# A transformer layer with attention and routed experts on one core: a new order of transfers at the start, and gates stored in pieces of four bytes

## The chip, the cores and the metric

One core of a Trainium2 chip runs the whole kernel. The metric is the device time of one execution in microseconds. A core has TensorE (PE, matrix products into eight PSUM banks), VectorE (DVE), ScalarE (ACT), GpSimd (POOL) and SyncE (SP), each with an instruction list of its own, and 16 DMA engines between DRAM and SBUF. The lists run beside each other and meet at semaphores.

## The reference, cut to what matters

```
x: (8, 512, 128);  xn = layernorm(x)
attention over 16 heads of 8, keys and queries turned by an angle that depends on the batch index:
    scores = q k^T / sqrt(8);  weights = softmax(scores);  att = weights v
router on xn: s = sigmoid(xn gate_w^T); group scores of 8 groups of 4 (sum of the best two of s + e_bias);
    the best 4 groups; in them the best 6 experts of s + e_bias;
    combine = 2.5 * s / sum of the chosen s (zero for the other experts)       (tokens x 32 experts)
moe = sum over e of ((relu(xn up_e^T))^2 * combine_e) down_e^T                 (32 experts, inner 64)
shared = (relu(xn shared_up^T))^2 shared_down^T                                (inner 256)
out = x + att + moe + shared
```

All arithmetic is in fp32.

## The kernel before

**Units and steps.** Each of the 8 batches of 512 tokens is cut into 16 units, so there are 128 units; a unit `u` treats two experts (128 inner columns) of batch `u // 16` and, for attention, four heads and one block of 128 keys (`kt = u % 4`). Four units with the same four heads are a step; there are 32 steps, and a step has 16 score tiles for the row maxima, which run ahead of use by up to 12 tiles (`SC_AT`). In a unit TensorE's list is: the first couple of heads (`couple(u, 0)`: `weights_max` adds the negated maxima as a product of `ones` with `m_rows`, `weights_product` the scores), some score tiles for later maxima, `pv` of the unit before, then at most a few extra products for coming batches (at the unit numbers in the constants `X_UNIT`, `Q_UNIT`, `GATE_UNIT` and so on), the second couple, the down products (`expert_down`, up to two a unit by `DOWN_AT`, from unit 6 on), and the up product (`expert_up`), into the bank `up_b`, which the extra products share.

**The gates.** VectorE computes the router in ten pieces (`route`, at the units in `ROUTE_MID` and `ROUTE_END`; `ROUTE1_*` for batch 1). Its last piece writes `gates`, 128 tokens by 4 tiles by 32 experts. TensorE turns it with four transposes (`gate_transpose`) in unit 12, ScalarE copies the result to `gT` (`gate_out`), SyncE stores it to DRAM as `gate_rows` (experts by tokens, `store_gates`), and after that has landed, loads rows of it, each spread over 64 partitions, into `gate_at` (`load_gates`, one group of four units at a time, two buffers). POOL multiplies: `gated = gate_at * relu`, `g = gated * relu`. ScalarE makes `relu` from `up_b`, and the exponentials `probs` from the banks `st0` and `st1`.

**The stacks.** Queries and keys are split by POOL into a high and a low part (`split`), stored to DRAM (`store_rows`, four transfers of 256 KB each for q and k) and loaded in a stacked form (`load_stack`) as four rows groups per head. A row maximum is cut into three bf16 parts by POOL (`cut_max`), turned by TensorE, copied by ScalarE to `m_parts` and loaded by SyncE as `m_rows` (`load_max`, three small transfers).

**SyncE's order.** All transfers are issued by SyncE in one list, in order, waits included. In step `s` it sends `load_max(s + 1)`, `load_gates(s + 1)`, and, depending on the step, outputs, x and stores for the batch after the next, then `load_stack` for the next batch. `load_stack(1, ...)` waits until all eight stores of batch 1 have landed. For batch 0 the first two steps' stacks are made without DRAM; those of steps 2 and 3 go through it.

**The start.** Before unit 0 TensorE computes 16 score tiles for step 0; after the pair `i` of them it does one other product if `BESIDE` names it, and then six tiles of step 1 with the products in `BEHIND`. ScalarE evacuates in the same order. The exponential's table is loaded by a small `Exp` on `blank` after all of them.

**The end.** After unit 127 come the last down products, the last `pv`, the copy of its result, its turning, the last down product, and on VectorE `att_out`, then `last_sum`: x + att, then the accumulated bank on top.

## Time and profile before

| what | us |
|---|---|
| median of two runs | 665.76 (665.56 to 665.96) |
| the profiled execution | 666.02 |
| its span, from first to last instruction | 664.2 |

Mean granted TensorE clock over the span: 0.981 of full speed. Times in the rows count from the start of the span. In a timeline a row stands for one instruction or for neighbours of the same kind, with their count behind an x; the number in brackets is how long the engine stood idle before it, and what ended that.

### The profile page before, as it was taken

The page shows a single profiled execution, that of the slowest core. Times are in us where ns is not written, and L with a number is a line of the kernel's source. Part 1 is how long each engine was busy: PE and PEld are TensorE (multiplying, and loading weights), DVE is VectorE, ACT ScalarE, POOL GpSimd, SP SyncE. Part 2 cuts the span into 40 slices and gives each one's busy share as a digit, 9 for nine tenths or more (in the row PEclk, how much of TensorE's full clock was granted, in tenths as well). Part 3 has the DMA queues.
Part 4 walks back from the last instruction along what each step waited for, and adds up shares of the span by engine and source line. Part 5 has one row for each costly group of instructions (what it writes and reads, how often), then busy time and mean ns, then how long its engine had stood idle before and what let it go on. Part 6 is the DMA issues. An engine that isn't in the chain of part 4 may idle for free.

```text
span 664.2 us, 12408 instructions
## 1 busy us (share of the span) xinstructions
PE 643.2 (97%) x4320; PEld 297.6 (45%) x4320; DVE 421.3 (63%) x1056; ACT 410.5 (62%) x785; POOL 446.3 (67%) x528
## 2 busy tenths in 40 slices
PE   8897799999999999999999999999999999999996
PEld 5432444454444444444444444444444444444443
DVE  7785677485756767575765757575765867565402
ACT  3564365576666666676667666665676667666653
POOL 6730568876788677876688667875766667566653
PEclk9977799899999999999999999999999999999999
DMA  4444634532546443263545524273544524232420
GB/s 137 136 124 126 137 96 100 163 106 55 142 100 215 106 114 96 63 206 87 144 101 176 144 64 116 68 221 96 129 101 117 180 72 115 72 91 65 97 65 17
DMA packets 51966, 75.69 MB, mean 114 GB/s; under 512 B 5952, under 2 KB 19136, under 8 KB 51904
## 3 DMA queue, kind: packets, MB, share of 16 engines
q1 hardware_dynamic: 51904, 74.90, 42.2%
q8 instruction: 35, 0.57, 0.4%
q14 instruction: 27, 0.22, 0.1%
HBM read 56.14 MB, written 18.35 MB: 112 GB/s over the span
## 4 chain that ended last, share of the span: by engine, by line
PE 86%; POOL 6%; DMA 2%; issue 2%; SPq 1%; DVE 1%; ACT 1%; POOLq 0%; DVEq 0%
PE acc L1054 21%; PE pv L1048 18%; PE upb L1098 15%; PE st L1018 12%; PE st L1023 5%; PE sc L1007 4%; POOL gated L478 2%; POOL g L482 2%; PE upb L971 2%; PE upb L935 2%; PE upb L990 1%; DMA gate_at<-gate_rows 1%; PE upb L966 1%; PE upb L930 1%; PE upb L984 1%
## 5 line engine op out<-in xcount | busy, mean ns | idle before, releaser
L819 DVE TENSOR_REDUCE nmax<-sc 128x1 f32<-128x512 f32 x512 | 329.2, 686 | 195.7 <-PE sc L1007 193.9
L612 ACT ACTIVATE probs<-st 128x512 f32<-128x512 f32 x512 | 277.7, 594 | 57.4 <-PE st L1023 56.8
L478 POOL TENSOR_TENSOR gated<-gate_at,relu 128x512 f32<-128x512 f32 x127 | 161.9, 1275 | 138.4 <-ACT relu L617 132.0
L482 POOL TENSOR_TENSOR g<-gated,relu 128x512 f32<-128x512 f32 x127 | 161.5, 1271 | 25.8 <-PE acc L1054 7.8
L617 ACT ACTIVATE relu<-upb 128x512 f32<-128x512 f32 x128 | 76.5, 598 | 126.2 <-PE upb L1098 126.2
L1054 PE MATMUL acc<-dn,g 128*128 128x128 f32 x1016 | 147.6, 289 | 6.2 <-POOL g L482 6.2
L1023 PE MATMUL st<-stacks 32*128 32x512 f32 x512 | 152.2, 580 | 0.0
L1054 PEld LDWEIGHTS acc<-dn,g 128*128 128x128 f32 x1016 | 123.9, 193 | 48.6 <-issue 46.4
L1048 PE MATMUL pv<-probs,v_aug 128*32 128x512 f32 x1024 | 138.1, 612 | 0.0
L1007 PE MATMUL sc<-stacks 32*128 32x512 f32 x512 | 134.3, 497 | 1.0 <-DVE nmax L819 0.8
L1098 PE MATMUL upb<-xnT,up 128*128 128x512 f32 x256 | 133.5, 604 | 0.1
L1018 PE MATMUL st<-m_rows,ones 3*128 3x512 bf16 x512 | 106.4, 388 | 4.6 <-DMA m_rows<-m_parts 3.8
L1018 PEld LDWEIGHTS st<-m_rows,ones 3*128 3x128 bf16 x512 | 27.6, 91 | 148.4 <-issue 75.3
L1007 PEld LDWEIGHTS sc<-stacks 32*128 32x128 f32 x512 | 50.8, 184 | 9.7 <-DVE nmax L819 7.4
L1023 PEld LDWEIGHTS st<-stacks 32*128 32x128 f32 x512 | 51.2, 195 | 0.0
L1098 PEld LDWEIGHTS upb<-xnT,up 128*128 128x128 f32 x256 | 39.3, 194 | 3.3 <-issue 2.5
L1048 PEld LDWEIGHTS pv<-probs,v_aug 128*32 128x32 f32 x1024 | 20.2, 108 | 44.6 <-issue 44.3
L279 POOL CAST n_parts<-nmax 128x16 bf16<-128x16 f32 x32 | 6.4, 199 | 28.0 <-DVE nmax L819 28.0
L1054 PEld LDWEIGHTS acc<-sdn,sh 128*128 128x128 f32 x128 | 16.7, 205 | 11.7 <-ACT relu L617 11.7
L466 POOL TENSOR_TENSOR qk_parts<-qk,qk_parts 128x512 fp32r<-128x512 f32 x16 | 20.3, 1270 | 0.3
L1054 PE MATMUL acc<-sdn,sh 128*128 128x128 f32 x128 | 19.3, 299 | 0.0
L849 DVE TENSOR_TENSOR low_part<-gate_at,relu 128x512 f32<-128x512 f32 x1 | 0.7, 692 | 27.2 <-ACT relu L617 27.2
(151 smaller groups left out, 417.5 us busy)
## 6 DMA issues: line engine op xcount, KB each, us to landing
gate_at<-gate_rows SPq DMA_DIRECT2D x64, 512.0 KB, 6.7
stacks<-q_stack SPq DMA_DIRECT2D x30, 256.0 KB, 5.3
stacks<-k_stack SPq DMA_DIRECT2D x30, 256.0 KB, 6.0
q_stack<-qk_parts SPq DMA_DIRECT2D x28, 256.0 KB, 6.7
k_stack<-qk_parts SPq DMA_DIRECT2D x28, 256.0 KB, 6.0
x_res<-in_x SPq DMA_DIRECT2D x8, 256.0 KB, 7.1
out<-y SPq DMA_DIRECT2D x8, 256.0 KB, 6.9
m_rows<-m_parts SPq DMA_DIRECT2D x96, 4.0 KB
```

What stands on the lines that cost most here:

```text
L466: nc.gpsimd.tensor_tensor(qk_parts[:, w, 1, :], src, qk_parts[:, w, 0, :].bitcast(F32), ALU.subtract).then_inc(lo_ready, 1)
L478: nc.gpsimd.tensor_tensor(gated[:, u % 2, :], gate_at[:, group % RING, u % GATES, :], relu[:, u % RELUS, :], ALU.mult).then_inc(gated_read ...
L482: nc.gpsimd.tensor_tensor(g[:, u % 2, :], gated[:, u % 2, :], relu[:, u % RELUS, :], ALU.mult).then_inc(g_ready, 1)
L612: nc.scalar.activation(probs[:, u % 2, h, :], st_b[h % 2][:], ACT.Exp).then_inc(probs_ready, 1)
L617: nc.scalar.activation(relu[:, u % RELUS, :], up_b[:], ACT.Relu).then_inc(relu_ready, 1)
L819: nc.vector.tensor_reduce(out=nmax[:, s % 2, at:at + 1], in_=sc_b[tile % SC_BANKS][:], op=ALU.max, axis=AXX, negate=True).then_inc(s_read, 1)
L1007: nc.tensor.matmul(sc_b[tile % SC_BANKS][:], stacks[rows_of(h), s % NQ, 0, qt * P:(qt + 1) * P], stacks[rows_of(h), s % NQ, 1, :], start=T ...
L1018: nc.tensor.matmul(st_b[h % 2][:], ones[max_rows_of(h), :], m_rows[max_rows_of(h), u // TT % 2, :], start=True, stop=False)
L1023: nc.tensor.matmul(st_b[h % 2][:], stacks[rows_of(h), j, 1, kt * P:(kt + 1) * P], stacks[rows_of(h), j, 0, :], start=False, stop=True).the ...
L1048: m = nc.tensor.matmul(pv_b[h * VW:(h + 1) * VW, :], columns[:, at:at + VW], probs[:, u % 2, h, :], start=kt == 0 and first, stop=kt == TT ...
L1054: m = nc.tensor.matmul(acc_b[:, t * P:(t + 1) * P], src[:, t * P:(t + 1) * P], weights, start=first and t == 0, stop=end, skip_group_check ...
L1098: nc.tensor.matmul(up_b[:], up[:, n * P:(n + 1) * P], xnT[:, b * T:(b + 1) * T], start=True, stop=True).then_inc(up_done, 1)
```

## The change

1. **Gates of batches 1 to 7.** TensorE no longer turns them and ScalarE no longer copies them. ScalarE stores `gates` itself, from its own DMA queue, at the end of units 11 (tiles 0 and 1) and 12 (tiles 2 and 3), after the unit's last exponential. Each of the four transfers of a batch writes 128 x 32 elements of 4 bytes, each to a place of its own in the rows of `gate_rows`. `gate_stored` counts them, and `load_gates` waits for all four. Batch 0 goes the old way.
2. **SyncE's order at the start.** `load_max(0)` comes ahead of the stores of batch 0's rows. `store_parts(1)` and `load_x(3)` move behind the first two gate loads in step 0. The loads of group 0 are cut in two halves with a semaphore each.
3. **Order of products at the start.** `BESIDE`, `BEHIND` and two new entries, `CUT_WAIT` and `LAST`, give a new order; the shared products and k of batch 1 come behind the transpose of the first maxima. The last six warming matmuls (`WARM_CUT`) go. The exp table is loaded right after the first maxima's copy.
4. **POOL's order at the start.** The second stacks and the first `cut_max` come ahead of batch 0's splits; the clearing of the third `v` buffer ahead of `cut_max(1)`. For batch 3, `inverse_std` and `normalise` come in units 8 to 11 in place of 11 to 14. `V1_UNIT`, `Q2_UNIT` and `ROUTE1_*` move by some units. From unit 9 on the units with two down products are the odd ones, where they were the even ones.
5. **The end.** x of the last batch is added by TensorE into the accumulating bank, as a product with the identity (`add_x`, in unit 124), and VectorE's first sum goes. The last down product comes ahead of the last turning.

```diff
--- before.py
+++ after.py
@@ -86,7 +86,7 @@
         due = u - LAG + 1
-        n = 2 if u >= FIRST_LAG + 2 and u % 2 == 0 else 1
+        n = 2 if u >= FIRST_LAG + 3 and u % 2 else 1
         while done < due and n:
@@ -173,7 +173,7 @@
         m_ld = [sem(f"m_ld{j}") for j in range(NQ)]
-        gate_ld = [sem(f"gate_ld{i}") for i in range(RING)]
+        gate_ld = [sem(f"gate_ld{i}") for i in range(RING)]; gate_first = sem("gate_first")
         stored_2 = sem("stored_2"); stored = sem("stored")
@@ -205,34 +205,35 @@
         sum_ready = sem("sum_ready"); y_ready = sem("y_ready")
-        last_gated = sem("last_gated"); last_g = sem("last_g"); last_rest = sem("last_rest")
+        last_gated = sem("last_gated"); last_g = sem("last_g")
         ATT_KT, MAX_KT, CUT_KT = 1, 2, 1
         CUT0_UNIT = {4: 3, 10: 4}
-        X_UNIT, V_UNIT, Q_UNIT, K_UNIT, SH_UNIT, GATE_UNIT = 0, (3, 11), 4, 8, (7, 15), 12
-        V1_UNIT, GATE0_UNIT, X2_UNIT, Q2_UNIT, V2_UNIT = (0, 5), 4, 1, 3, (11, 13)
+        X_UNIT, V_UNIT, Q_UNIT, K_UNIT, SH_UNIT, GATE_UNIT = 0, (3, 11), 4, 8, (7, 15), (11, 12)
+        V1_UNIT, GATE0_UNIT, X2_UNIT, Q2_UNIT, V2_UNIT = (0, 3), 4, 1, 5, (11, 13)
         SHDOWN_UNIT = (5, 13)
...
         STATS_UNIT, AGGR_UNIT, LN_UNIT, NORM_UNIT = 10, 11, 11, (12, 13, 14, 14)
+        LN0_UNIT, NORM0_UNIT = 8, (9, 10, 11, 11)
         ROUTE_MID, ROUTE_END = {0: 0, 3: 3, 4: 4, 7: 6, 8: 7}, {1: 1, 2: 2, 6: 5, 8: 8, 10: 9}
-        ROUTE1_MID, ROUTE1_END = {6: 0, 7: 2, 8: 4, 10: 6, 11: 8}, {6: 1, 7: 3, 8: 5, 10: 7, 11: 9}
+        ROUTE1_MID, ROUTE1_END = {4: 0, 6: 2, 7: 4, 8: 6, 10: 8}, {5: 1, 6: 3, 7: 5, 8: 7, 10: 9}
         ROUTE0_MID, ROUTE0_END = {0: 3, 1: 5, 2: 7, 3: 9}, {0: 4, 1: 6, 2: 8}
         SIGMOIDS = 1
-        WARM_FIRST, WARM_COPY, WARM_ROWS, WARM_CUT = 15, 3, 3, 3
-        BESIDE = {0: ("q", 0), 1: ("k", 0), 3: ("rows", 1), 4: ("rows", 0), 6: ("v", 0), 7: ("x", 1), 8: ("shared", 0)}
-        BEHIND = {2: ("shared", 1), 3: ("q", 1), 4: ("k", 1)}
+        WARM_FIRST, WARM_COPY, WARM_ROWS = 15, 3, 3
+        BESIDE = {0: ("rows", 1), 2: ("rows", 0), 4: ("q", 0), 6: ("x", 1), 7: ("v", 0), 8: ("k", 0)}
+        CUT_WAIT, BEHIND, LAST = ("q", 1), {2: ("shared", 0), 4: ("shared", 1)}, ("k", 1)
         NW1, NW2, NUP, NDN = 4, 3, 2, 2
@@ -325,22 +326,27 @@
                                  m_parts[k * TILES:(k + 1) * TILES, :]).then_inc(m_ld[s % NQ], 16)
-            def store_gates(b):
+            def store_gates():
+                b = 0
                 sp.wait_ge(gT_ready, b + 1)
...
                 if j == 0:
-                    sp.wait_ge(gate_stored, (b + 1) * 16)
+                    sp.wait_ge(gate_stored, 16 + b * (TT * 16))
                 if group == 0:
...
                 wait(sp, g_ready, (group - RING + 1) * GATES)
-                for e in range(EPS):
-                    sp.dma_start(gate_at[e * EI:(e + 1) * EI, group % RING, :, :],
-                                 gate_dram[b * NE:(b + 1) * NE, :].rearrange("(j n e) t -> j e n t", n=GATES, e=EPS)[j, e]
-                                 .partition_broadcast(EI)).then_inc(gate_ld[group % RING], 16)
+                halves = ((slice(0, GATES // 2), gate_first), (slice(GATES // 2, GATES), gate_ld[0]))
+                for units, loaded in halves if group == 0 else ((slice(0, GATES), gate_ld[group % RING]),):
+                    for e in range(EPS):
+                        sp.dma_start(gate_at[e * EI:(e + 1) * EI, group % RING, units, :],
+                                     gate_dram[b * NE:(b + 1) * NE, :]
+                                     .rearrange("(j n e) t -> j e n t", n=GATES, e=EPS)[j, e, units]
+                                     .partition_broadcast(EI)).then_inc(loaded, 16)
             def load_residual(b):
@@ -363,27 +369,26 @@
                 sp.dma_start(up[:, half_at], upT[:, half_at]).then_inc(up_ld, 16)
+            load_max(0)
             for w in range(2):
                 store_rows(0, w, slice(2 * QUAD, H), stored_2)
-            load_max(0)
             load_stack(0, 2)
...
             sp.dma_start(dn[:], down.rearrange("(n p) d -> p n d", p=P)).then_inc(dn_ld, 16)
-            store_parts(1)
-            load_x(FIRST_X)
             load_residual(0)
...
                 if s + 1 < STEPS:
-                    if j == NQ - 1:
-                        store_gates(b + 1)
                     load_max(s + 1)
                     if s == 0:
-                        store_gates(0)
+                        store_gates()
                         load_gates(0)
                     load_gates(s + 1)
+                    if s == 0:
+                        store_parts(1)
+                        load_x(FIRST_X)
                 if j == 1:
@@ -473,7 +478,9 @@
                 pool.wait_ge(relu_ready, u + 1)
-                if u % GATES == 0:
+                if u == 0:
+                    pool.wait_ge(gate_first, EPS * 16)
+                elif u == GATES // 2 or u % GATES == 0:
                     pool.wait_ge(gate_ld[group % RING], (group // RING + 1) * (EPS * 16))
@@ -500,18 +507,18 @@
             normalise(1, range(TT))
-            for k in range(4):
-                split(0, k)
             second_stack(1)
...
             cut_max(pool, nc.gpsimd, 0)
+            for k in range(4):
+                split(0, k)
             normalise(2, range(TT))
...
                 square(0, i)
+            set_v(2)
             cut_max(pool, nc.gpsimd, 1)
...
                 split(1, k)
-            set_v(2)
             cut_max(pool, nc.gpsimd, 2)
@@ -529,9 +536,9 @@
                 if b + FIRST_X < B:
-                    if n == LN_UNIT:
+                    if n == (LN_UNIT if b else LN0_UNIT):
                         inverse_std((b + FIRST_X,), (b + 1) * LN_STEPS)
-                    tiles = [k for k in range(TT) if NORM_UNIT[k] == n]
+                    tiles = [k for k in range(TT) if (NORM_UNIT if b else NORM0_UNIT)[k] == n]
                     if tiles:
@@ -600,9 +607,15 @@
                 nc.scalar.activation(m_parts[:], up_b[0:MAX_PARTS * TILES, 0:P], ACT.Copy).then_inc(m_ready, 1)
+            def store_gates(b, tiles):
+                act.wait_ge(gates_ready, b + 1)
+                for t in tiles:
+                    act.dma_start(gate_dram[b * NE:(b + 1) * NE, t * P:(t + 1) * P].rearrange("e p -> p e"),
+                                  gates[:, t, :], allow_slow_non_contiguous=True).then_inc(gate_stored, 16)
             def gate_out(b):
                 act.wait_ge(gate_turned, b + 1)
-                wait(act, gate_stored, b * 16)
                 nc.scalar.activation(gT[:, :], up_b[0:NE, :], ACT.Copy).then_inc(gT_ready, 1)
@@ -630,7 +643,7 @@
             logits_out(0)
-            for kind, i in tuple(BESIDE.values()) + (("max", 0),) + tuple(BEHIND.values()):
+            for kind, i in tuple(BESIDE.values()) + (("max", 0), CUT_WAIT) + tuple(BEHIND.values()) + (LAST,):
                 if kind == "v":
@@ -643,8 +656,9 @@
                     max_rows(0)
-            act.wait_ge(sigmoid_set, 1)
-            nc.scalar.activation(blank_out[:], blank[:, 0:1], ACT.Exp).then_inc(exp_set, 1)
+                    act.wait_ge(sigmoid_set, 1)
+                    nc.scalar.activation(blank_out[:], blank[:, 0:1], ACT.Exp).then_inc(exp_set, 1)
             for u in range(UNITS):
@@ -663,8 +677,6 @@
                         shared_relu(b + 1, SH_UNIT.index(n))
-                    if n == GATE_UNIT:
-                        gate_out(b + 1)
                 if b + 2 < B:
@@ -676,6 +688,9 @@
                 exponent(u, 3)
+                if b + 1 < B and n in GATE_UNIT:
+                    k = GATE_UNIT.index(n)
+                    store_gates(b + 1, (2 * k, 2 * k + 1))
             att_evac(STEPS // PAIR - 1)
@@ -805,7 +820,9 @@
                     then(nc.vector.tensor_scalar(wsum[:, 1, :], wsum[:, 0, :], ROUTED_SCALE, None, ALU.mult))
-                    wait(dve, gate_turned, b)
+                    if b:
+                        dve.wait_ge(gate_turned, 1)
+                        dve.wait_ge(gate_stored, 16 + (b - 1) * (TT * 16))
                     nc.vector.tensor_tensor(gates[:], tmp[:],
@@ -854,14 +871,11 @@
             def last_sum():
-                dve.wait_ge(x_res_ld, B * 16)
                 dve.wait_ge(atty_ready, B * NQ)
-                nc.vector.tensor_tensor(y[:, 0, :], x_res[:].rearrange("p t d -> p (t d)"),
-                                        att_y[:].rearrange("p t j c -> p (t j c)"), ALU.add).then_inc(last_rest, 1)
-                dve.wait_ge(last_rest, 1)
                 dve.wait_ge(down_done, B * SLICES)
                 dve.wait_ge(y_stored, (B - 1) * 16)
-                nc.vector.tensor_tensor(y[:, 1, :], acc_b[:], y[:, 0, :], ALU.add).then_inc(y_ready, 1)
+                nc.vector.tensor_tensor(y[:, 1, :], acc_b[:], att_y[:].rearrange("p t j c -> p (t j c)"),
+                                        ALU.add).then_inc(y_ready, 1)
             nc.vector.memset(blank[:], 1.0).then_inc(blank_ready, 1)
@@ -1066,6 +1080,13 @@
                 down_slice(src, dn[:, n, :], n == 0, n == SLICES - 1).then_inc(down_done, 1)
+            def add_x():
+                pe.wait_ge(x_res_ld, B * 16)
+                for t in range(TT):
+                    nc.tensor.matmul(acc_b[:, t * P:(t + 1) * P], ident[:], x_res[:, t, :],
+                                     start=False, stop=False, skip_group_check=True)
             def shared_down(b, i):
@@ -1086,8 +1107,6 @@
                         pe.wait_ge(sh_relu, (b + 1) * NSH + SH_UNIT.index(n) + 1)
-                    if n == GATE_UNIT:
-                        pe.wait_ge(gT_ready, b + 2)
                 if b + 2 < B:
@@ -1102,14 +1121,14 @@
                     pe.wait_ge(w2_ld, NW2 * 16)
-                    pe.wait_ge(sig_ready, 1)
+                    pe.wait_ge(xnT_ready, 2)
                     make_v(i)
...
                 elif kind == "x":
-                    pe.wait_ge(v_ready, 1)
+                    pe.wait_ge(sig_ready, 1)
                     transpose_x(i)
@@ -1136,16 +1155,17 @@
             beside(*BESIDE[TILES // 2])
-            pe.wait_ge(sh_relu, 1)
-            warm(WARM_CUT, st_b[0])
-            pe.wait_ge(xnT_ready, 2)
+            beside(*CUT_WAIT)
+            pe.wait_ge(v_ready, 1)
             max_transpose(0)
...
                     beside(*BEHIND[i])
+            beside(*LAST)
             pe.wait_ge(m_ready, 1)
             pe.wait_ge(sh_relu, NSH)
+            pe.wait_ge(v_ready, 1)
             pe.wait_ge(qk32_ready, 4)
@@ -1166,8 +1186,6 @@
                         shared_up(b + 1, SH_UNIT.index(n))
-                    if n == GATE_UNIT:
-                        gate_transpose(b + 1)
                 if b + 2 < B:
@@ -1177,6 +1195,8 @@
                     shared_down(b, SHDOWN_UNIT.index(n))
+                if u == UNITS - TT:
+                    add_x()
                 if u == UNITS - 1:
@@ -1194,9 +1214,9 @@
             pv(UNITS - 1)
+            expert_down(UNITS - 1)
             pe.wait_ge(relu_ready, UNITS)
             att_transpose(STEPS // PAIR - 1)
-            expert_down(UNITS - 1)
 # ---- launch: one core ----
```

## Rows read from the trace of the kernel before

**Rows 1.** The page's list of engines: busy us, share, instructions.
```profile
PE 643.2 (97%) x4320; PEld 297.6 (45%) x4320; DVE 421.3 (63%) x1056; ACT 410.5 (62%) x785; POOL 446.3 (67%) x528
```

**Rows 2.** The page's costliest groups: count, busy, mean ns; idle before, releaser.
```profile
L478 POOL TENSOR_TENSOR gated<-gate_at,relu 128x512 f32<-128x512 f32 x127 | 161.9, 1275 | 138.4 <-ACT relu L617 132.0
...
L1054 PE MATMUL acc<-dn,g 128*128 128x128 f32 x1016 | 147.6, 289 | 6.2 <-POOL g L482 6.2
```

**Rows 3.** Timeline of TensorE, 25 to 124 us: start, us, what, idle before.
```profile
25.07 0.94 PE L948 MATMUL st<-blank 128*128 128x128 f32 x6 [0.69 <-ACT sh L595]
...
34.69 2.07 PE L1098 MATMUL upb<-xnT,up 128*128 128x512 f32 x2
...
56.81 0.61 PE L1018 MATMUL st<-m_rows,ones 3*128 3x512 bf16 x2 [3.75 <-DMA m_rows<-m_parts]
...
74.81 2.05 PE L1054 MATMUL acc<-dn,g 128*128 128x128 f32 x8 [4.63 <-POOL g L482]
...
85.66 0.39 PE L1018 MATMUL st<-m_rows,ones 3*128 3x512 bf16 x2
...
123.08 1.77 PE L1054 MATMUL acc<-dn,g 128*128 128x128 f32 x8 [1.59 <-POOL g L482]
```

**Rows 4.** Windows: stretch, busy by engine, granted TensorE clock, DMA share, GB/s.
```profile
34.70:41.50 6.80, 6.80 (x28) 2.37 (x27) 4.53 (x20) 2.90 (x6) 0.00 (x0) 0.50 0.29 83
55.20:62.00 6.80, 5.19 (x25) 1.94 (x25) 1.89 (x3) 1.67 (x3) 0.00 (x0) 0.50 0.04 10
123.40:126.90 3.50, 3.50 (x16) 1.90 (x14) 0.00 (x0) 0.30 (x1) 3.36 (x4) 0.51 0.78 186
31.50:53.00 21.50, 20.82 (x95) 7.59 (x95) 18.26 (x64) 13.50 (x26) 6.55 (x13) 0.84 0.55 172
190.00:266.00 76.00, 76.00 (x536) 34.70 (x532) 50.98 (x131) 50.27 (x98) 55.91 (x66) 1.00 0.47 124
45.00:55.20 10.20, 7.81 (x34) 2.53 (x33) 8.63 (x25) 5.25 (x10) 5.16 (x8) 1.00 0.84 255
```

**Rows 5.** Timeline of SyncE's transfers, 28 to 69 us.
```profile
30.84 0.85 SPq L372 DMA_DIRECT2D dn<-in_down  x1
...
52.99 1.78 SPq L325 DMA_DIRECT2D m_rows<-m_parts  x3
...
61.75 0.35 SPq L330 DMA_DIRECT2D gate_rows<-gT  x1
...
63.40 2.61 SPq L341 DMA_DIRECT2D gate_at<-gate_rows  x4
...
66.88 1.42 SPq L317 DMA_DIRECT2D stacks<-k_stack  x1
```

**Rows 6.** DMA issues and queue 1: 63.4 to 72; 200 to 203.5; 1.7 to 4 us.
```profile
gate_at<-gate_rows SPq DMA_DIRECT2D x4, 512.0 KB, 8.6
...
q1 hardware_dynamic: 60, 0.01, 1.7%
...
q1 hardware_dynamic: 1033, 0.46, 74.3%
```

**Rows 7.** Timeline of ScalarE, around 31 us and in batch 1.
```profile
31.38 1.28 ACT L647 ACT_TABLE_LOAD   x1
...
188.72 0.60 ACT L617 ACTIVATE relu<-upb 128x512 f32<-128x512 f32 x1 [0.69 <-PE upb L1098]
...
212.48 0.60 ACT L617 ACTIVATE relu<-upb 128x512 f32<-128x512 f32 x1 [0.86 <-PE upb L1098]
```

**Rows 8.** Groups by line and shape: the turning of the gates.
```profile
L977 PE MATMUL upb<-ident,gates 128*32 128x128 f32 x32 | 5.3, 292 | 0.9 <-DVE gates L809 0.9
```

**Rows 9.** Timeline of SyncE: the gate loads for batch 2's first group.
```profile
202.34 1.28 SPq L341 DMA_DIRECT2D gate_at<-gate_rows  x2
```

**Rows 10.** Groups by line and shape: VectorE's first sum at the end.
```profile
L859 DVE TENSOR_TENSOR y<-x_res,att_y 128x512 f32<-128x512 f32 x1 | 0.7, 693 | 0.1
```

## Prediction

> **What bounds the kernel now.** I read the page's engine list first: the matmul engine is busy 97% of the span [rows 1], no other engine over 67%. So time comes back only where TensorE stands still, where it runs at half its clock, or where its own work is taken away. Next the costliest groups with what ended the idle time before them: TensorE's down products stood 6.2 us for POOL's g [rows 2], and the timeline of TensorE shows these as two stops, with one more of 3.75 us for m_rows [rows 3]; no other stop of it after the start reaches 1 us. The windows give the clock: 34.7 to 41.5, 55.2 to 62.0 and 123.4 to 126.9 us stand at half of the full clock, the 1.2 GHz level in place of 2.4, and a fourth stretch like them at 72.2 to 79.1; in a whole batch of the steady part (190 to 266 us) it is 1.00 with TensorE busy for all of the 76.0 us [rows 4]. Three of the four begin in or just after a stop, of 3.75, 4.63 and 1.59 us [rows 3]. The first stop is at unit 4 (one unit is one pass of the loop over 128), the second inside unit 6, the third in unit 15. After that nothing but its own work bounds TensorE. Hence two questions: what becomes of the first 130 us, and what does one steady batch cost.
>
> Why unit 4 stopped: SyncE's list. It first sent the eight stores of batch 1's stacks, for which it waited on POOL's splits, then x_next and x_res, and the three m_rows pieces only at 52.99 us [rows 5], though these rows had been ready since unit 2. Why unit 6 stopped: gates of batch 0 stored at 61.75, four gate_at loads from 63.40 us [rows 5] that took 8.6 us each in the median to land [rows 6], then two POOL operations; the first down product began at 74.81 us [rows 3].
>
> **The change, part by part (profiled execution: 664.2 span, 666.0 us in all, which is 0.2 above the median of 665.8).**
>
> *1, up to unit 4.* The maxima leave the exp table load (31.38 us, 1.28 us, [rows 7]) on the chain into the first exp; now it stands before the last projections, so 1.3 us go. The six warming records, 0.94 us, and the 0.69 us stop for sh_relu before them go too [rows 3]; VectorE's 16 maxima, which run beside, give back only about 1.2 of these, I estimate. I expect the first up product at 32.2 instead of 34.7 us. Against that, the stores of batch 0's rows now queue behind m_rows 0; they go out from about 27 to 32 us, land at about 35, and the stacks of step 2 land near 38, just when unit 2 wants them: 0 to 1.5 us lost, I take 0.5. From there VectorE sets the pace: it was busy 18.26 of the 21.5 us from 31.5 to 53.0 [rows 4], for units 0 to 3, and its work stays. So unit 4 starts 18 us after 31, at 49 (bounds 48 to 51), where it was 56.81 [rows 3]; its m_rows are sent at unit 2 and should be there, the 3.75 us stop is gone. The project of q moves from unit 3 to unit 5 at no cost in sum.
>
> *2, unit 4 to unit 8.* Gates of batch 0 are turned in unit 4 as before. Their store was issued 4.9 us into the unit [rows 3, 5], much of that at half clock; I take 3.4, so 52.4, and from store to first load were 1.65 us [rows 5]: loads start at 54. Now the first two bring half a group each and land after some 3 us (512 KB at the 200 GB/s of the old ones), g of unit 0 is ready near 59.6 after two 1.27 us operations [rows 2]; TensorE reaches its use at 60.4. The stop of 4.63 us goes. But now comes the queue: behind the six gate loads (2 MB) stand the eight stores (2 MB) and x_next, and behind them load_stack of batch 1, which waits on SyncE until all eight stores have landed, and behind that m_rows 2, which unit 8 needs. SyncE issues the loads 54 to 58, the stores to 63. The four loads of before, 2.1 MB issued in 2.6 us, took 8.6 us each to land [rows 5, 6]: 2.1 MB in 10.6 us or so, 200 GB/s; while the stores ran, the DMA moved 255 GB/s over 10.2 us with its slow start in it, so nearer 300 [rows 4]. So the last store lands at 72 (54 + 10 + 7, and x_next within; bounds 67 and 74), stack issues 1.3 us, m_rows 1.8, landing 1: 76. TensorE would be at unit 8 by 69.5 (49, two units of 4.5, 6.4 for unit 6 with three down products, 5.1). A new stop of 6.5 us (bounds 1.5 and 9). Unit 8 starts at 76, was 85.66 [rows 3]: gain 9.7.
>
> *3, unit 8 to 16.* The 0.9 us that TensorE stood before the gates of batch 1 [rows 8] and the 1.59 us for g with its 3.5 us at half clock (worth 1.7) go [rows 3, 4], since POOL starts its chain 15 us earlier. The inverse deviation now comes in unit 8, but it waits for VectorE's moments of unit 11, so POOL stands for some us; counted forward with 2.55 us for a gating [rows 2], g of units 9 to 13 come out 1 us before to 0.5 us after their use: cost 0 to 2, I take 0. After the new stop I expect a new stretch at half clock as after the two old ones (5.2 us of the second were busy [rows 4]): half is 2.6. Net gain 1.6.
>
> *4, gates of batches 1 to 7.* The 32 turning matmuls make 5.3 us of busy time, 0.66 for the four of a batch [rows 8]; the last one's end overlaps the next product, so I take 0.54 (bounds 0.5 and 0.66). 28 go. Seven times 0.54 is 3.8 us off TensorE, which has no gap there. ScalarE instead issues two transfers at the end of unit 11 and two at the end of unit 12. Its relu comes after, and before that relu it stood 0.69 us [rows 7]; nothing else covers it, as unit 12 now has no extra product. The price of an issue on ScalarE is not in the trace. On SyncE 0.65 us was usual for gate loads, 0.85 for the 2048 pieces of dn, and one issue behind a full queue took 1.42 us [rows 5]. Below nothing is excluded, each is an added instruction. I take 0.5: 2 x 0.5 less 0.7 is 0.3 in unit 12, and in unit 13 the shared product covers it. Seven times 0.3 is 2.1 us. Net gain 1.7.
>
> Time to land: 4 x 4096 pieces are 1024 for each of the 16 DMA engines. The nearest rows: 60 small packets took 1.7% of 16 engines over 3.5 us, 16 ns each (256 bytes mostly); 1033 packets, nearly all of 512 bytes, took 74.3% over 2.3 us, 26.5 ns each [rows 6]. A piece of 4 bytes moves less, so I take 16 ns, bounds 8 and 26.5: 16.4 us. Covered: from relu 11 at 188.7 to SyncE's gate_at load at 202.3 us are 13.6 [rows 7, 9]; the load then lands near 209 while relu of unit 16 begins at 212.5 [rows 7], 3.7 more, and its down product runs a unit after g, another 3.7. So 21 us, 20.5 ns a piece, cost nothing. What this hides under is that distance; without it each ns more costs 1 us a batch.
>
> The Trainium skill speaks against this part: its page "DMA: Bandwidth & Descriptors" (Rules for kernel authors) says a strided last dimension becomes one descriptor per element and that a rearranged pattern is 19 times slower than a transposing transfer. No row here has such a store. Taken on the 1.65 us from the old store of 64 KB to the first load [rows 5] it would give, as an estimate, 31 us a batch, 10 beyond what is covered, and some 724 us in all. My sum does not use it.
>
> *5, the end.* x is added in unit 124 as four products shaped like a down product: 147.6 us over 127 of these is 1.16 [rows 2], less some overlap 1.1. VectorE's sum of 0.69 us [rows 10] goes. The last down product moves into the gap in which TensorE waits for ScalarE's copy of the last output, and overhangs it by some 0.1. Net loss 0.5.
>
> Sum: -9.7 - 1.6 - 1.7 + 0.5 = -12.5. From 666.0: **653.5 us**.
>
> **Rivals.**
> *A, ScalarE is held by its own issues* (slower). If ScalarE cannot go on until most of the 256 pieces per engine are written out, an issue takes h us. TensorE then loses 4h - 2.1 us in a batch (covers 0.7 at unit 12, 1.4 at unit 13), 28h - 14.7 in seven. Without part 4's loss the sum is 651.4. It decides at h = 1.05 us, where the whole gain is spent. For it: SyncE's issues grew with a full queue, and 4096 pieces are twice the dn transfer. Against: dn returned in 0.85. With h = 1.4, the row's: 676; with 1.8: 687.
> *B, the pieces land late.* At 26.5 ns, 27.1 us, 6 late in each batch, 42 in all: 695. For it: nothing here has pieces that small written to DRAM. Against: 16 ns for 256 bytes. The rule of the Trainium skill's page above points to this rival, and further out.
> *C, the queue takes back the front.* Stores and loads interfere as in 63 to 77 us, the wait at unit 8 is 9 us, POOL's order costs 2: gain 4.5 less, 658; with unit 4 not before 51, 660.
> *D, no wait at unit 8*, stores at 350 GB/s beside the loads: 4 to 7 us and the half clock saved: 645 to 648.
>
> **Chances.** Forecast (647 to 658) 0.50, A 0.20, B 0.10, C 0.10, D 0.10. The range leaves out B and the half of A with h above 1.6 (681): 644 to 681. Two per cent, about what a measurement tells from no change here, are 13.3 us, so 652.4 is the border to faster: the forecast sits on it. Faster over 2%: D and 0.23 of the forecast, 0.33. Slower over 2% (679): B and 0.11 of A, 0.21. The rest, 0.46.
>
> **What would show it.** In the waits: no wait for g in unit 6 and for m_rows in unit 4, but one for m_rows at unit 8 near 70 to 76 us. In the clock: a low stretch there, none at 123. In a steady batch: 75.9 us become 75.7; TensorE's gaps appear only before unit 12's second pair of products. If ScalarE's issues take over 1 us, A; if POOL waits for gate_at once in each batch and SyncE's issue of gate_at comes over 14 us after relu 11, B. Wrong altogether if the first up product isn't earlier than 34, or unit 4 waits for the stacks or maxima.

## The result

The changed kernel takes 1120.4 us in the median of two runs (1115.2 and 1125.7) against 665.8: 1.687 times the time before, 95% interval 1.676 to 1.698. The forecast was 653.5, and its range ended at 681. The profiled execution took 1115.2, its span 1113.4 us. In the experiments below some executions of e2, e3 and e9, the profiled ones among them, ran more than 1.5% above the fastest of their kernel at a lower clock, so the ratios leave them out and e2 has none.

From the page of the changed kernel: the engine list, TensorE's busy tenths and clock in 40 slices, ScalarE's DMA queue, and the group of the down products.

```profile
PE 699.2 (63%) x4294; PEld 326.3 (29%) x4294; DVE 422.6 (38%) x1055; ACT 407.1 (37%) x778; POOL 446.5 (40%) x528
...
PE   9988205795258941589415794155962599305998
...
PEclk8998558698578975789757797576986799657899
...
q10 hardware_dynamic: 115136, 0.46, 64.4%
...
L1068 PE MATMUL acc<-dn,g 128*128 128x128 f32 x1016 | 163.0, 310 | 0.1
```

To be read beside [rows 1]: TensorE is busy 699.2 us in place of 643.2, of 1113.4. Its idle time went from 21.0 to 414.2 us; that is 393.2 of the 449.2 us by which the span grew, and the other 56.0 are work at a lower clock. The tenths show seven holes, one for each batch whose gates go the new way. The new queue q10 holds 115,136 packets in 0.46 MB, and their records come to 64.4% of 16 engines' time: 0.644 x 16 x 1113.4 / 115,136 is 99.6 ns, the mean duration of the record of one piece of 4 bytes. Records overlap, so this is not the time for which a piece occupies an engine. From 103 to 170 us the queue's row is

```profile
q10 hardware_dynamic: 12891, 0.05, 148.9%
```

By the time that passed these are 67 x 16 / 12,891 = 83 ns a piece and engine, by their records 124 ns.

TensorE's waits over the whole span (total, times, longest):

```profile
PE acc L1068 <- ACT relu L630: 171.7, 6, 32.5
PE st L1032 <- ACT probs L625: 93.5, 7, 14.9
PE st L1032 <- DMA m_rows<-m_parts: 91.7, 8, 16.3
PE upb L980 <- ACT relu L630: 41.7, 1, 41.7
```

306.9 us are waits for ScalarE and 91.7 for m_rows. ScalarE's timeline at units 11 and 12 of batch 0 shows why:

```profile
102.79 0.43 ACTq L614 DMA_DIRECT2D gate_rows<-gates  x1
...
103.25 16.38 ACTq L614 DMA_DIRECT2D gate_rows<-gates  x1
119.72 0.60 ACT L630 ACTIVATE relu<-upb 128x512 f32<-128x512 f32 x1 [15.89 <-issue]
...
122.42 26.18 ACTq L614 DMA_DIRECT2D gate_rows<-gates  x1
...
148.64 20.04 ACTq L614 DMA_DIRECT2D gate_rows<-gates  x1
168.78 0.60 ACT L630 ACTIVATE relu<-upb 128x512 f32<-128x512 f32 x1 [45.51 <-issue]
```

The first store is issued in 0.43 us, as on SyncE. The second holds ScalarE's list for 16.4 us, the third for 26.2, the fourth for 20.0. relu of unit 11 comes 15.9 us late and relu of unit 12 45.5 us late (before, it stood 0.69, [rows 7]), and TensorE, which cannot reuse `up_b`, stands. SyncE's list, just after:

```profile
177.78 1.85 SPq L326 DMA_DIRECT2D m_rows<-m_parts  x3
202.25 1.28 SPq L346 DMA_DIRECT2D gate_at<-gate_rows  x2
```

After the maxima at 177.8 it waits until 202.3 us for the stores to land, where in a steady batch before 13.6 us from relu 11 to this load were enough [rows 7, 9]. The maxima themselves, three transfers of 4 KB, are held up as long: TensorE, which needs them, goes on at 202.29 us after a stop of 16.26 us.

The start, which the change reorders, by TensorE's timeline:

```profile
36.98 1.13 PE L1117 MATMUL upb<-xnT,up 128*128 128x512 f32 x2
...
51.87 0.52 PE L1032 MATMUL st<-m_rows,ones 3*128 3x512 bf16 x2
...
64.89 1.13 PE L1068 MATMUL acc<-dn,g 128*128 128x128 f32 x8
...
73.45 1.02 PE L1117 MATMUL upb<-xnT,up 128*128 128x512 f32 x2
78.91 0.61 PE L1032 MATMUL st<-m_rows,ones 3*128 3x512 bf16 x2 [4.44 <-DMA m_rows<-m_parts]
```

It answers to [rows 3]: the first up product at 36.98 (was 34.69), unit 4 at 51.87 (56.81) without a stop, the first down product at 64.89 (74.81) without a stop, and unit 8 at 78.91 (85.66) after a stop of 4.44 us for m_rows.

### The profile page after: what moved, and what is told of

Read it like the earlier page. It is cut to its first block, busy times and chain, and to the rows that moved or that the text cites. A ratio compares the mean times of both kernels' runs of the same rounds, so it can differ in the third digit from the quotient of the medians.

```text
span 1113.4 us, 12360 instructions
## 1 busy us (share of the span) xinstructions
PE 699.2 (63%) x4294; PEld 326.3 (29%) x4294; DVE 422.6 (38%) x1055; ACT 407.1 (37%) x778; POOL 446.5 (40%) x528
## 3 DMA queue, kind: packets, MB, share of 16 engines
q10 hardware_dynamic: 115136, 0.46, 64.4%
## 4 chain that ended last, share of the span: by engine, by line
PE 45%; issue 18%; DMA 15%; ACTq 13%; DVE 3%; another core or an unknown queue 2%; ACT 2%; SPq 2%; POOL 1%; DVEq 0%; POOLq 0%
ACTq L614 13%; PE acc L1068 11%; PE pv L1062 9%; DMA m_rows<-m_parts 9%; PE upb L1117 7%; PE st L1032 7%; DMA gate_rows<-gates 4%; PE st L1037 3%; PE sc L1021 2%; DVE nmax L836 1%; DMA gate_at<-gate_rows 1%; PE upb L949 1%; ACT probs L625 1%; SPq L326 1%
## 5 line engine op out<-in xcount | busy, mean ns | idle before, releaser
L1032 PE MATMUL st<-m_rows,ones 3*128 3x512 bf16 x512 | 115.0, 416 | 186.3 <-ACT probs L625 93.5
L1037 PE MATMUL st<-stacks 32*128 32x512 f32 x512 | 165.0, 627 | 0.0
L1068 PE MATMUL acc<-dn,g 128*128 128x128 f32 x1016 | 163.0, 310 | 0.1
L1068 PEld LDWEIGHTS acc<-dn,g 128*128 128x128 f32 x1016 | 138.4, 212 | 49.0 <-issue 45.1
L1021 PE MATMUL sc<-stacks 32*128 32x512 f32 x512 | 146.1, 535 | 3.0 <-DVE nmax L836 2.8
L1062 PE MATMUL pv<-probs,v_aug 128*32 128x512 f32 x1024 | 144.3, 637 | 0.0
L1117 PE MATMUL upb<-xnT,up 128*128 128x512 f32 x256 | 141.4, 636 | 0.5 <-ACT qk L566 0.3
L1068 PE MATMUL acc<-sdn,sh 128*128 128x128 f32 x128 | 23.7, 344 | 171.7 <-ACT relu L630 171.7
L980 PE MATMUL upb<-wvg,xnT 128*128 128x160 f32 x56 | 12.0, 339 | 41.7 <-ACT relu L630 41.7
L980 PEld LDWEIGHTS upb<-wvg,xnT 128*128 128x128 f32 x56 | 8.4, 198 | 53.1 <-ACT relu L630 51.0
```

The source lines that it names most:

```text
L1021: nc.tensor.matmul(sc_b[tile % SC_BANKS][:], stacks[rows_of(h), s % NQ, 0, qt * P:(qt + 1) * P], stacks[rows_of(h), s % NQ, 1, :], start=T ...
L1032: nc.tensor.matmul(st_b[h % 2][:], ones[max_rows_of(h), :], m_rows[max_rows_of(h), u // TT % 2, :], start=True, stop=False)
L1037: nc.tensor.matmul(st_b[h % 2][:], stacks[rows_of(h), j, 1, kt * P:(kt + 1) * P], stacks[rows_of(h), j, 0, :], start=False, stop=True).the ...
L1062: m = nc.tensor.matmul(pv_b[h * VW:(h + 1) * VW, :], columns[:, at:at + VW], probs[:, u % 2, h, :], start=kt == 0 and first, stop=kt == TT ...
L1068: m = nc.tensor.matmul(acc_b[:, t * P:(t + 1) * P], src[:, t * P:(t + 1) * P], weights, start=first and t == 0, stop=end, skip_group_check ...
L1117: nc.tensor.matmul(up_b[:], up[:, n * P:(n + 1) * P], xnT[:, b * T:(b + 1) * T], start=True, stop=True).then_inc(up_done, 1)
```

## The experiments

Each run's time is the median of its executions, and each ratio is to the kernel before on the same chip in the same rounds. That kernel took 663.4 us beside e1 to e4, 668.4 beside e5, e6, e7 and e10, 664.5 beside e8, e9 and e11, and 665.8 beside e12 to e14, so runs of different sets are compared by their ratios.

### The two halves apart: e1_front and e2_gates

e1 takes the gates back to TensorE and SyncE, and keeps the rest of the change. e2 is the opposite. From e1's edit against the changed kernel:

```diff
-                if b + 1 < B and n in GATE_UNIT:
-                    k = GATE_UNIT.index(n)
-                    store_gates(b + 1, (2 * k, 2 * k + 1))
...
+                    if n == GATE_UNIT:
+                        gate_out(b + 1)
...
+                    if n == GATE_UNIT:
+                        gate_transpose(b + 1)
...
+                    if j == NQ - 1:
+                        store_gates(b + 1)
```

> The changed kernel with the gates of batches 1 to 7 turned by TensorE and stored by SyncE again; all else of the change stays. Theory S (the four stores of 4-byte pieces a batch cost everything): 655 us, from the 12.5 us forecast less the 1.7 of the gates. Rival F (the new order of the front also lost time, since the trace of the changed kernel shows a stretch at half clock at 21 to 28 us and a stop of 4.4 us before unit 8): 662 to 668.

> The kernel before with nothing changed but the way of the gates of batches 1 to 7. Theory S: the whole loss, 1120 to 1140 us, as the front's gain is missing. Rival F: below the changed kernel's 1120.

Measured: e1 663.1 us, ratio 0.9988 (0.9958 to 1.0018). e2 1190 us (1151 to 1200), which is above theory S's 1120 to 1140 and not below, as rival F had it. So the way of the gates alone makes the loss, and theory S holds for that. But e1 isn't at 655: rival F was right about the front (662 to 668). TensorE's waits in e1, and two windows in which its clock was down, with the same window of before under them:

```profile
PE st L1024 <- DMA m_rows<-m_parts: 4.4, 1, 4.4
PE acc L1060 <- POOL g L490: 3.7, 4, 1.3
PE sc L1013 <- DVE nmax L828: 2.1, 4, 1.0
```

```profile
20.00:26.70 6.70, 6.29 (x18) 3.83 (x18) 4.49 (x11) 1.35 (x3) 2.02 (x7) 0.50 0.01 2
81.30:84.70 3.40, 3.40 (x10) 0.57 (x10) 1.73 (x7) 1.68 (x3) 0.00 (x0) 0.50 1.05 238
```

```profile
20.00:26.70 6.70, 5.37 (x29) 3.21 (x29) 4.47 (x11) 2.76 (x6) 6.24 (x10) 1.00 0.43 150
```

Before, that stretch ran at full clock and TensorE has 29 product records in it; in the new order it has 18, at half clock. The smaller number is in part the low clock's own effect. In the 6.5 us ahead of the stretch, still at full clock, TensorE was busy 5.71 us with 16 records in e1 and 6.11 us with 18 before. It is the new order at the very start that brings this: in nine profiles with it (the changed kernel, e1, e4 to e8, e10, e11) the stretch stands at 0.50 to 0.75, in four with the old one (before, e12 to e14) at 1.00. That order is of products, of POOL's work and of `load_max(0)`, and no run takes these three apart. With that the first maxima are turned at 27.72 us (before, 25.94), and the first up product comes at 36.87, later than before (34.69), not earlier.

### Held issue or late landing: e3_side and e6_one

e3 is e1 plus four such stores a batch, from a constant tile, for which nobody waits but ScalarE, once, at its very end:

```diff
+                for t in tiles:
+                    act.dma_start(side_dram[b * NE:(b + 1) * NE, t * P:(t + 1) * P].rearrange("e p -> p e"),
+                                  ident[:, 0:NE], ...).then_inc(side_stored, 16)
```

> e1_front plus four stores a batch by ScalarE in the same places, of the same shape (4096 pieces of 4 bytes each), read from a constant tile and written to DRAM rows that nobody reads; the computation is whole. Theory H (ScalarE is held by its own issues): 14 holds, 62 us a batch as in the changed kernel (16.4 + 26.2 + 20.0), so at least 655 + 7 x 60 = 1075 us. Rival L (SyncE's wait for the stores is what costs, forecast's rival B): ScalarE goes on at once and the time is near 660. In the changed kernel both stood; the wait adds what e3 lacks to 1120.

Measured: 1201 us (1174 to 1231), ratio 1.775 (1.757 to 1.793). Nothing in the computation waits for these stores, and still the whole loss is there, so SyncE's wait for their landing isn't needed for it: theory H. TensorE's waits in e3:

```profile
PE acc L1071 <- ACT relu L632: 217.2, 6, 41.1
PE st L1035 <- DMA m_rows<-m_parts: 142.6, 8, 28.1
PE upb L994 <- ACT relu L632: 115.3, 7, 22.7
```

e6 sends only the first of the four.

> e3_side with one store a batch (4096 pieces, end of unit 11) in place of four. Theory H (an issue returns in 0.43 us when the queue is empty, and is held only behind an unfinished one): 7 issues at 0.4 us, at most the pieces' traffic in the way of others; 663 to 672. Rival T (the traffic of the pieces itself slows the other transfers): 20 us of busy DMA a batch delay m_rows and the stacks: 680 or more.

Measured: 812.3 us, ratio 1.213. Its issue, TensorE's wait for m_rows in sum and once in full, and the landing of the one store that SyncE itself sent in the window from 108 to 140 us:

```profile
108.34 0.42 ACTq L615 DMA_DIRECT2D side_rows<-ident  x1
```

```profile
PE st L1035 <- DMA m_rows<-m_parts: 99.7, 8, 17.1
```

```profile
124.57 2.31 SPq L328 DMA_DIRECT2D m_rows<-m_parts  x3
```

```profile
144.22 0.61 PE L1035 MATMUL st<-m_rows,ones 3*128 3x512 bf16 x2 [9.19 <-DMA m_rows<-m_parts]
```

```profile
gate_rows<-gT SPq DMA_DIRECT2D x1, 64.0 KB, 30.2
```

ScalarE is free at once, as H says, yet H's 663 to 672 us are missed: some 0.214 of the time before, 142 us, are lost. Rival T (680 or more) is right too, with a price that I had not thought of: SyncE's small transfers stand behind the pieces. Batch 1's gate store took 30.2 us to land (in e1 such a store takes 1.9 in the median), three m_rows transfers issued at 124.57 us let TensorE go on only at 144.22, and TensorE waited 99.7 us in all for m_rows (4.4 in e1). So there are two mechanisms. An issue of 4096 pieces returned at once when no such store was unfinished (0.42 us in e6, seven times) and was held when one was (16.4 us above). And the pieces hold up the other queue on the same DMA engines. The Trainium skill's page "DMA: Bandwidth & Descriptors" (Issuing engines are not separate DMA queues) says that transfers issued by different engines run on the same 16 DMA engines and interleave; this trace agrees, with SyncE's 30.2 us beside ScalarE's pieces.

### What makes a piece slow: e4_lines, e10_apart, e7_sbuf, e5_eight, e11_whole

All are e3 with another destination:

```diff
-   e3   side_dram[b * NE:(b + 1) * NE, t * P:(t + 1) * P].rearrange("e p -> p e")
+   e4   side_dram[(b * TT + t) * P:(b * TT + t + 1) * P, :, 0]
+   e10  side_dram[b * NE:(b + 1) * NE, t * P:(t + 1) * P, 0].rearrange("e p -> p e")
+   e7   side_sb[:, (b - 1) * TT + t, :, 0]
+   e5   side_dram[b * NE // 2:(b + 1) * NE // 2, t * P:(t + 1) * P, :].rearrange("e p c -> p e c")
+   e11  side_dram[(b * TT + t) * P:(b * TT + t + 1) * P, :]
```

The last dimension of `side_dram` has 16 floats in e4 and e10, of which one is written, and 2 in e5; `side_sb` is a tile in SBUF with every second float written.

> e3_side with each piece of 4 bytes written to a place of its own, 64 bytes from the next, so that no two pieces share 64 bytes. Theory C (pieces of neighbouring partitions fall into the same bytes of DRAM around them and wait for each other; half of the pieces took 9 ns, some over 500): a hold falls from 20 us to about 4096 / 16 x 10 ns = 2.6 us, the whole to under 700 us. Rival N (any write of 4 bytes to DRAM is slow): as e3_side within 5%.

> e3_side with the same turned order (a partition's pieces go to 32 different rows) but every piece 64 bytes from the next, as in e4_lines. Theory C (shared 64 bytes cost): as e4_lines, 780 to 800. Rival O (it is the order, each next piece of a partition far from the last, that costs): as e3_side, 1200.

> e3_side with the 4096 pieces of 4 bytes written 8 bytes apart into a tile in SBUF in place of DRAM. Theory W (the write into DRAM costs, not the piece): a store takes 4096 / 16 x 9 ns = 2.3 us, holds of about 2 us, the whole 663 to 690. Rival G (making and moving 4096 pieces costs): e4_lines' 788 or more.

> e3_side with pieces of 8 bytes, half as many (2048 a store), two experts side by side. Theory P (each write of a small piece costs, whatever its bytes): the holds halve, the excess over e1_front falls from 538 us to about 270: 930 us. Rival Q (the 64 bytes around a piece are what is rewritten, each as often as pieces fall in it): also half as many writes per 64 bytes, and the same 930; if bytes counted: as e3_side, 1200.

> e1_front plus four stores a batch by ScalarE of the same bytes as in e3_side, but with each partition's 32 values side by side, 128 pieces of 128 bytes a store. Theory H: two issues of 0.43 us at the end of units 11 and 12, 0.2 us of it not covered: e1_front + 1 to 2 us. Rival (any transfer issued by ScalarE costs as much as the products that it replaces, 3.8 us): + 4 us or more.

The row of queue q10 (packets, MB, share of 16 engines' span) in e3, e5, e4, e10, e7 and e6, in this order:

```profile
q10 hardware_dynamic: 115136, 0.46, 63.1%
```

```profile
q10 hardware_dynamic: 57792, 0.46, 24.1%
```

```profile
q10 hardware_dynamic: 115136, 0.46, 30.5%
```

```profile
q10 hardware_dynamic: 115136, 0.46, 24.3%
```

```profile
q10 hardware_dynamic: 115136, 0.46, 8.0%
```

```profile
q10 hardware_dynamic: 28784, 0.12, 17.5%
```

| run | pieces of a batch, where | us | ratio to before | span | mean ns of a record |
|---|---|---|---|---|---|
| e3 | 16,384 of 4 B, DRAM, 16 of them in 64 bytes | 1201 | 1.775 | 1229.3 | 107.8 |
| e5 | 8,192 of 8 B, DRAM, 8 in 64 bytes | 813 | 1.214 | 814.5 | 54.3 |
| e4 | 16,384 of 4 B, DRAM, 64 bytes apart | 788 | 1.185 | 785.2 | 33.3 |
| e10 | the same, in the turned order | 770 | 1.150 | 770.1 | 26.0 |
| e7 | 16,384 of 4 B, SBUF | 705 | 1.053 | 702.6 | 7.8 |
| e6 | 4,096 of 4 B, as e3 | 812 | 1.213 | 815.8 | 79.4 |
| e11 | 512 of 128 B | 665 | 1.001 | 660.0 | |

The last column is share x 16 x span / packets; as records overlap, it serves to compare the runs. Theory C holds in its direction: with every piece in 64 bytes of its own a record falls from 108 to 26 ns although the order of writing is the same (e10 against e3), so rival O falls, and so does rival N (e4 is a third under e3, not within 5%). But it isn't all: e4 was expected under 700 us and took 788, and e10 took 770. A 4-byte write into DRAM at 26 to 33 ns is still three to four times one into SBUF at 7.8 ns. That is theory W's direction, but e7's 705 us lie between its 690 and rival G's 788. And e5 refutes both halves of its expectation: with half the pieces there is left not half of e3's excess over e1 but 28% of it (0.215 of 0.776 by the ratios), since the record of each halved as well. That a piece costs the more, the more neighbours it has in the same 64 bytes, 108, 54 and 26 ns for 16, 8 and 1, fits the three runs; the mechanism in the memory is not shown by them, nor that 64 bytes is where it ends, since only distances of 4, 8 and 64 bytes were tried, and with them the distance between two successive pieces of a partition grew too (2, 4 and 32 KB). With one store alone (e6) a record took 79.4 ns in place of 107.8, so the number of stores under way may count as well.

The holds follow the same prices. In e7, where pieces are cheap, a pair of issues in batch 1 and, for comparison, e11's pair of 128-piece stores:

```profile
188.78 0.63 ACTq L615 DMA_DIRECT2D side_sb<-ident  x1
...
189.45 5.42 ACTq L615 DMA_DIRECT2D side_sb<-ident  x1
```

```profile
187.10 0.84 ACTq L615 DMA_DIRECT2D side_rows<-ident  x2
```

Even at 7.8 ns a piece the second issue holds ScalarE for 5.4 us (5.4 to 7.2 over the batches; the fourth, at the end of unit 12, for 2.2 to 3.1), and e7 loses 0.054 of the time before, 36 us. TensorE's waits for relu are 26.7 us of it. With 128 pieces both issues together take 0.84 us, although the first is not yet written out when the second is issued, and e11 is not to be told from e1 (ratio 1.0008, 0.9975 to 1.0042, e1's own 0.9988 on another chip): theory H's 1 to 2 us fit, and the rival's 4 us lie at the edge of what the intervals allow. TensorE waited for no relu in e11. So what costs is the count of pieces and where they fall, and not ScalarE as issuer.

The delay of the other queue goes with slow pieces too. TensorE's waits for m_rows are 142.6 us in e3 and 99.7 in e6, but 4.1 in e10 and 4.2 in e7, as in e1 (4.4), though the 64 KB gate store still needed 8.5 us in e10. In e10 and e7 the stops that TensorE has beyond e1's are those for ScalarE's relu.

### The front: e8_max, e9_list, e12_table, e13_units, e14_tail

e8 is e1 with one load moved: `load_max(2)` ahead of `load_x(3)` and of the stack loads that wait. e9 starts from the kernel before and changes SyncE's list alone (with the halves of the first gate loads and POOL's waits for them, not shown here), with that same load ahead:

```diff
-            store_parts(1)
-            load_x(FIRST_X)
             load_residual(0)
...
                     load_gates(s + 1)
+                    if s == 0:
+                        store_parts(1)
+                        load_max(2)
+                        load_x(FIRST_X)
```

> e1_front with the load of m_rows for step 2 issued ahead of x_next and of the stack loads that wait for batch 1's stores. Theory M (the 4.4 us stop before unit 8, with the 3.4 us at half clock after it, is the queue's doing): 6 us less than e1_front: 657. Rival K (POOL's chain takes over: it must reach g of units 9 to 15 in time, and inverse_std waits for unit 11's moments): under 2 us less, and the gain shows up as waits of TensorE for g.

> The kernel before with SyncE's list alone changed: batch 1's stores and x_next behind the first gate loads, these in two halves, and m_rows for step 2 ahead of x_next. Order of products, POOL's order, the table load, the gates' way and the end are those of before. Theory M: the stops of 3.75 and 4.63 us and the 4.7 us lost at half clock behind them go, nothing takes their place: 650 to 655. Rival K: POOL, which starts earlier but has the same work up to unit 16, ends near the same time: 660 or more.

Measured: e8 658.5 us, ratio 0.9907 (0.9877 to 0.9938), e9 655.5 us, 0.9860 (0.983 to 0.989). The moved load is worth 0.8% or 5.4 us: theory M, near its 6, and no wait for m_rows is left in e8. e9 comes out at the upper end of its 650 to 655. The kernel before with the new list is at least as good as the whole new front; the intervals of e8 and e9 overlap, and only e12, below, lies clear of e8. Added to e9, one at a time: the early table load (e12); on that, the change's unit numbers and POOL's early normalising (e13); and, on e12, the new end (e14).

> e9_list with the exp table loaded right after the first maxima's copy, in ScalarE's gap before the second shared product. Theory X (the load stands on the path into the first exponential): 1.3 us less than e9_list, ratio 0.984. Rival (VectorE sets the pace of the first units anyway): 0 to 0.5 us, ratio 0.986.

> e12_table with the change's numbers of units and POOL's early normalising of batch 3: double down products in odd units, the v half in unit 3, q in unit 5, routing of batch 1 some units earlier, inverse_std in unit 8. Theory K (POOL stands before unit 11's moments, and this costs as much as the earlier work brings): within 1 us of e12_table. Rival E (the early work frees units 12 to 15, where TensorE waited for g): 3 us less. What is left between this and e8_max is the order at the very start and the end.

> e12_table with the change's end: x added by TensorE in unit 124, one sum less on VectorE, the last down product ahead of the last turning. Forecast: 0.5 us slower than e12_table. Rival: 0.3 us faster, since in the changed kernel without the gates (e1_front) the end lost and gained 0.8 us each.

| run | us | ratio to before | span and clock of the profiled execution |
|---|---|---|---|
| e12 | 653.5 | 0.9817 (0.9775 to 0.9859) | 650.9, 0.999 |
| e13 | 657.8 | 0.9878 (0.9831 to 0.9926) | 653.0, 0.997 |
| e14 | 654.1 | 0.9840 (0.9796 to 0.9883) | 651.6, 0.996 |

The windows of before's low stretches, in e12, and its waits:

```profile
34.70:41.50 6.80, 6.51 (x40) 2.31 (x43) 6.46 (x30) 4.78 (x10) 0.42 (x2) 1.00 0.51 133
55.20:62.00 6.80, 6.67 (x49) 2.51 (x48) 5.09 (x9) 5.33 (x12) 1.94 (x5) 1.00 0.68 164
...
123.40:126.90 3.50, 3.50 (x33) 1.83 (x28) 2.75 (x7) 2.45 (x5) 2.85 (x5) 1.00 0.04 16
```

```profile
PE acc L1062 <- POOL g L490: 3.1, 2, 1.6
PE st L1026 <- DMA m_rows<-m_parts: 1.5, 1, 1.5
```

The stretches of [rows 4] stand at 1.00, and the stops of 3.75 and 4.63 us are gone; 1.5 us for m_rows and 3.1 for g are left. e12 is the best of all, 12.3 us under before; its interval leaves open whether that is over 2%. Against e9 it shows no gain of its own: the intervals overlap, and the five executions in e9's ratio have a median of 653.5 us, as e12's six. Its first exponential begins at 32.32 us where before's begins at 32.78, so the early table load brings some 0.5 us there: the rival's 0 to 0.5 and not 1.3. For e13 both expectations miss: it's 4.3 us above e12 in the median, 2.1 in the spans of the profiled executions; the intervals overlap, so this is likely and not shown. Its waits:

```profile
PE acc L1063 <- POOL g L491: 2.8, 3, 1.3
PE sc L1016 <- DVE nmax L828: 2.3, 5, 1.0
```

g costs hardly less than in e12 (2.8 us, 3.1 there), the 1.5 us for m_rows are gone, and 2.3 us of waits for VectorE's maxima are new, where the routing of batch 1 now stands earlier in VectorE's list. e14 is 0.6 us above e12 in the median and 0.7 in the span, with the forecast's sign and size, and inside the noise.

## Why the prediction was wrong

**The step that failed is part 4: the price of an issue, "I take 0.5", and with it the price of a piece, "so I take 16 ns, bounds 8 and 26.5".** The 0.5 us were right for the first store (0.43) and wrong for every one behind it, 9.0 to 26.2 us in the changed kernel, since I priced the call and not the room in the queue behind it. This alone would have been enough: e7's pieces took 7.8 ns, under my lower bound, and e10's 26.0 ns, inside the bounds, and still these runs took 705 and 770 us, beyond the range's 681. The second error made it worse. A piece's record took 99.6 ns, four times the upper bound. I reasoned that a smaller piece moves less and so can't cost more than the nearest row, a 512-byte one. But the rows at hand were pieces that share no 64 bytes with others, as in e10. What was not in the trace, and was the point of the change, is that 16 neighbours share 64 bytes: nearly four times e10's 26.0.

**Rival A had the mechanism and its formula.** The 28 issues of the changed kernel took 355 us, 12.7 in the mean (batch 1's four, shown above, are the longest, 15.8). So 28h - 14.7 gives 340 us, and TensorE's waits for ScalarE were 306.9. The sum 651.4 + 340 gives 992 us; the profiled execution took 1115. Of what is missing, 91.7 us are the waits for m_rows. So the rival's place, its cover and its count were about right, and its size was off by a factor of seven to nine, because its h of 1.4 to 1.8 us came from a row of SyncE (1.42 us) without any transfer of 4096 pieces. Rival B happened as well (the load at 202.3 us waited 22.6 us), but e3 shows that it isn't needed, and TensorE never waited for g behind it. I gave A a chance of 0.20, and no case of mine reached 1115. Missing from all of them was what e6 shows: small transfers of SyncE behind the pieces, some 14 us a batch.

The Trainium skill's rule (page "DMA: Bandwidth & Descriptors", Rules for kernel authors), by which I wrote 724 us, pointed the right way and is nearer than my 16 ns, and it still falls short. From the first issue of batch 1's gates to the first load, 31 us by my estimate, were 99 (102.79 to 202.25). The median gate store landed after 48.0 us, the same bytes in 128 pieces (e11) after 3.9, twelve times. The Trainium skill's factor of 19 is against a transposing transfer, which no run here has; that I put it on a plain store was my own step.

**Part 1 failed in its start.** The first up product was to come at 32.2 and came at 36.98, beyond the 34 that I had named as the sign of being wrong altogether. In this order TensorE's clock fell at 20 us, and I had counted no such loss: the first maxima were turned at 27.95 us, 2.0 later than before. From there to the first up product 9.03 us passed where 8.75 did before. Of the 1.3 us for the table load nothing shows, as TensorE now stood 1.09 us for ScalarE's last projection; with the load moved alone (e12) it is 8.40. Unit 4 came 2.9 us after my 49. **Part 2 held**: no stop for g, none at unit 4, and a new stop at unit 8 from m_rows behind the stores, 4.4 us where I wrote 6.5 (bounds 1.5 and 9), with half clock after it; from unit 4 to unit 8 27.0 us as forecast, and e8 takes the stop away. But with the late start unit 8 gained 6.8 in the changed kernel and 5.0 in e1, not 9.7. **Part 3 failed**: +1.6 forecast; in e1 the span is 3.4 us under before's, so 1.6 of the 5.0 were lost again behind unit 8, the loss at the end and the half clock at 81 to 85 us in it; TensorE waited for g four times, 3.7 us. **Part 5**: 0.5 forecast, 0.6 and 0.7 measured, inside the noise. The saving of 3.8 us by the missing transposes was never to be seen.

For the front my sum of 11.3 us stood against 0.3 us by medians and 3.4 by the spans (e1). The same list of transfers in the kernel before, with one load ahead, gives 9.0 us (e9), with the early table load 12.3 (e12). So the estimate of what the stops are worth was fair; what I gave the new order at the start was wrong in sign.

**Open.** Why 16 neighbours in 64 bytes cost four times one, and at which distance this ends; why e7's second issue is held 5.4 us when the 4112 records of a store, at 7.8 ns on 16 engines, make 2.0; what in the new order at the start lets TensorE's clock fall at 20 us, of which only the 5.71 busy us in place of 6.11 ahead of the fall are known; and whether e13 is really slower than e12.

## What to carry to other kernels

Price a transfer by its number of pieces and by how they fall in memory, not by its bytes: the records of one turned store of 16 KB to DRAM make some 20 us on 16 DMA engines (e6: 4112 of 79.4 ns), and turning a whole batch's gates on TensorE cost 0.66 us. An engine that also computes should not issue a transfer behind an unfinished one with thousands of pieces. And while pieces that share 64 bytes are under way, small and urgent transfers of another queue wait with them (e3, e6). When the price of an operation isn't in the trace, a bound from "the nearest row" holds only if that row shares what is new in the operation; here it was the neighbours, and one run of a side store would have shown it.

## What the runs showed of the hardware that I had not expected

- The record of a 4-byte piece takes 7.8 ns into SBUF (e7), 26 to 33 ns into DRAM alone in its 64 bytes (e10, e4), 54 (as 8 bytes) with 8 in them (e5), 79 to 108 with 16 (e6, the changed kernel, e3).
- The first issue of 4096 pieces returns in 0.42 to 0.68 us. The one right behind it held ScalarE for 5.4 to 7.2 us even with pieces into SBUF (e7), for 7.3 to 9.0 in e10 and 11.0 to 16.5 in the changed kernel.
- One such store a batch, its issuer free after 0.42 us, cost some 20 us a batch (e6), 14 of them in TensorE's waits for the other queue's m_rows.
- The five executions in e9's ratio lie in the order of their mean granted clock: 652.4 us at 0.999, 653.4 and 653.5 at 0.996, 655.5 and 655.6 at 0.991. So one and the same kernel moves by 3 us with the share of time that its clock stands low.
